# Two-layer transformer kernel: sixteen weighting steps of a batch joined into four, and a new order of all steps

## Chip, cores and metric

The kernel runs on one core of a Trainium2 chip. The metric is device time in microseconds. The engines are TensorE (PE), VectorE (DVE), ScalarE (ACT), GpSimd (POOL) and SyncE (SP), which issues most DMA copies.

## The reference

Sixteen batches of 512 tokens, 128 features, go through four layers: RWKV time and channel mixing; a soft decision tree of depth 8; causal attention with 16 heads of 8 dimensions and rotary positions; a mixture of 16 experts, of which two are picked per token. Each layer's output is added to its input and normalized. What the change touches is the attention's last part:

```python
scores = jnp.einsum('bthd,bshd->bhts', q, k) / jnp.sqrt(jnp.float32(dh))
scores = scores + causal[None, None, :, :]
weights = jax.nn.softmax(scores, axis=-1)
out = jnp.einsum('bhts,bshd->bthd', weights, v).reshape(b, seq, d)
```

## The kernel before

Each engine has a list of named steps in `ORDER`, such as `3:weigh0`. The number ahead of the name is a lag: in turn t of the loop the step works on batch t minus the lag. `run` goes through the list once per turn, so four or five batches are under way at once and an engine does its steps exactly in the written order. Semaphores join the engines: `until(engine, b, name, n)` makes an engine wait until n steps of that name of batch b are done. A step that waits holds up all that stands behind it on its engine.

The steps that matter here:

- `row0` to `row39` (TensorE): scores of queries against keys, in 40 units of up to 512 columns, each a `kh,qh` product and a `maskb,identb` product per piece, into two PSUM banks `S[0]`, `S[1]` in turn. `rowmax` (VectorE) takes the maxima and frees the bank; unit n waits for `rowmax` of unit n - 2. A unit of one piece is followed by the next step 0.28 us after its start, one of two pieces after 0.34 us.
- `score0` to `score39` (TensorE): the same products turned, keys by queries, with the maxima taken off, again into the two banks. `exp0` to `exp39` (ScalarE, line 525) writes the exponentials to one of ten slots of `prob` and frees the bank; unit n waits for `exp` n - 2. `exp` n with n of 10 or more waits for the `weigh` steps that read its slot ten units before.
- `weigh0` to `weigh15` (TensorE, tiles `prob,vaug`): exponentials times values. Step 4g + s handles group g of four heads, for one of the four blocks of keys. Its four matmuls use 32 columns of the array each (`tile_position`). A group needs ten `prob` slots.
- `pvT_out0` and `pvT_out1` (ScalarE) move the weighted sums out after 12 and 16 weighting steps; `back0`, `back1` (TensorE, tiles `ident,pvT`, line 958) turn them; `attend0`, `attend1` (VectorE) divide; then `attT`, `attn_out`.
- Time mixing of a batch two ahead: `k`, `v`, `r`, then `inverse0` to `inverse3` (VectorE reciprocals, line 732), `rwkv0` to `rwkv3` (GpSimd, line 409), `read_out0` to `read_out3` (TensorE, tiles `wo,inner`), `x2` (VectorE, line 742), `moments2`. `read_out0` needs all four `rwkv`.
- Channel mixing: `xn2T`, `cmk0` to `cmk3` (TensorE), each waiting for a `silu` (VectorE) of two before, `cmr`, `cmv0` to `cmv3`.
- Experts of the batch before: `gb0` to `gb15` and `expert0` to `expert15` (TensorE), `u` (VectorE for even numbers, GpSimd for odd ones behind `spread` on ScalarE).
- Rotary heads of the next batch: `xcT`, `rope0` to `rope3` (TensorE), `part_hi`, `part_mid` (ScalarE), `part_lo` (GpSimd), and `heads0`, `heads1` (SyncE): 18 copies each into `qh` and `kh`. `row0` needs all of `heads0`.

Besides these, `xbT`, `gates`, `leafT`, `leaf_sum` belong to the tree of the next batch, whose levels `tree0` to `tree7` are VectorE's; `moments`, `root` and `norm` to the normalizations; `maxT0`, `maxT1` put the maxima into the queries' rows.

Of the kernel before, what the change touches and what calls it, by code (L numbers as in the profile page):

```python
# [28 lines left out]
UNITS = 40  # L29
# [1247 lines left out]
```

How the kernel before makes its waits and increments, by code:

```python
        def until(eng, b, name, n=None):  # L112
            per = PER_BATCH[name]
            if b >= 0:
                eng.wait_ge(sems[name], b * per + (per if n is None else n))
# [1 line left out]
        def reached(eng, name, total):  # L118
            if total > 0:
                eng.wait_ge(sems[name], total)
# [181 lines left out]
        @block.sync  # L303
# [24 lines left out]
            def shared_bias(b):  # L328
                if b == 0:
                    sp.wait_ge(setup["bias_parts"], 7)
                    for i in range(PARTS):
                        sp.dma_start(bias_rows[i:i + 1, :], bias_part[i]).then_inc(setup["bias_in"], 16)
            load(0)
            for dst, src in GAINS:
                sp.dma_start(dst, src, allow_slow_non_contiguous=True).then_inc(setup["gains_in"], 16)
            for dst, src in FIRST[0::2]:
                sp.dma_start(dst, src, allow_slow_non_contiguous=True).then_inc(setup["first_loaded"], 16)
            for dst, src in TIME_LOADS[0:2]:
                sp.dma_start(dst, src, allow_slow_non_contiguous=True).then_inc(setup["time_loaded"], 16)
            for dst, src in LOADS:
                sp.dma_start(dst, src, allow_slow_non_contiguous=True).then_inc(setup["loaded"], 16)
            sp.wait_ge(setup["kh_ones"], 4)
            run("sp", {"load": lambda b: load(b + 1) if b + 1 < B else None, **each("heads", 2, spread_heads), **each("max_rows", 2, spread_maxima), "store": store, "shared_bias": shared_bias})
            until(sp, B - 1, "stored")
```

## Time and profile before

| | |
|---|---|
| median of 3 runs | 1709.79 us (1707.97 to 1712.36) |
| profiled execution | 1714.23 us, its span 1711.8 us |
| busy in the span | PE 1570.9 us, DVE 1418.7, ACT 1025.3, POOL 913.5 |
| mean granted TensorE clock | 0.959 |

The span is the time from the first to the last instruction of the profiled execution. Busy time on one engine can overlap with that on the others; for TensorE, matmuls are pipelined and a matmul's recorded end lies after the start of the next one. Where prices of TensorE's work are needed, differences of starts tell more than durations. A few matmul records are missing from the trace.

### The profile page before, as it was taken

The page shows a single profiled execution, that of the slowest core. Times are in us where ns is not written, and L with a number is a line of the kernel's source. Part 1 is how long each engine was busy: PE and PEld are TensorE (multiplying, and loading weights), DVE is VectorE, ACT ScalarE, POOL GpSimd, SP SyncE. Part 2 cuts the span into 40 slices and gives each one's busy share as a digit, 9 for nine tenths or more (in the row PEclk, how much of TensorE's full clock was granted, in tenths as well). Part 3 has the DMA queues.
Part 4 walks back from the last instruction along what each step waited for, and adds up shares of the span by engine and source line. Part 5 has one row for each costly group of instructions (what it writes and reads, how often), then busy time and mean ns, then how long its engine had stood idle before and what let it go on. Part 6 is the DMA issues. An engine that isn't in the chain of part 4 may idle for free.

```text
span 1711.8 us, 33755 instructions
## 1 busy us (share of the span) xinstructions
PE 1570.9 (92%) x12127; PEld 1094.8 (64%) x12205; DVE 1418.7 (83%) x3018; ACT 1025.3 (60%) x2110; POOL 913.5 (53%) x1233
## 2 busy tenths in 40 slices
PE   3566899999999999999999999999999999999976
PEld 1334558576766758676767768586767767584735
DVE  5776989899898989899998989898998989782612
ACT  3333475766666574857666575757666675746252
POOL 6445264746546574746556564746566474632303
PEclk9687899999999999999999999999999999999897
DMA  4002020110102020100102020201102020201000
GB/s 112 1 6 56 7 57 8 34 31 18 53 8 58 14 56 8 47 24 26 46 8 63 9 57 8 55 17 34 37 13 58 9 57 2 63 2 52 13 14 7
DMA packets 66969, 53.35 MB, mean 31 GB/s; under 512 B 8370, under 2 KB 65522, under 8 KB 66802
## 3 DMA queue, kind: packets, MB, share of 16 engines
q1 hardware_dynamic: 65650, 50.41, 10.7%
q8 instruction: 96, 1.57, 0.4%
q10 hardware_dynamic: 1152, 0.79, 0.2%
q14 instruction: 71, 0.58, 0.1%
HBM read 8.44 MB, written 4.19 MB: 7 GB/s over the span
## 4 chain that ended last, share of the span: by engine, by line
PE 77%; DVE 11%; ACT 3%; issue 3%; SPq 2%; POOL 2%; DMA 1%; another core or an unknown queue 0%; DVEq 0%; ACTq 0%; POOLq 0%
PE bank L962 73%; PE bank L958 4%; SPq L318 2%; DVE rall L788 2%; DVE rall L786 1%; DVE mixed L693 1%; DVE stats L684 1%; DVE rall L784 1%; ACT prob L525 1%; DVE inner L693 1%; DVE wkb L732 1%; DMA kh<-part 1%; DVE xc L814 1%; DVE mv L689 1%; ACT gT L525 0%
## 5 line engine op out<-in xcount | busy, mean ns | idle before, releaser
L525 ACT ACTIVATE prob<-bank 128x512 f32<-128x512 f32 x640 | 355.7, 597 | 131.7 <-PE bank L962 130.0
L962 PEld LDWEIGHTS bank<-wexpT,prob 128*128 128x128 f32 x2048 | 264.7, 193 | 29.2 <-issue 24.9
L962 PE MATMUL bank<-kh,qh 72*128 72x512 bf16 (+3 forms) x1024 | 250.6, 306 | 23.2 <-DVE rall L786 11.2
L962 PE MATMUL bank<-wexpT,prob 128*128 128x128 f32 x2048 | 265.6, 276 | 2.8 <-DVE prob L863 0.3
L461 POOL TENSOR_TENSOR prob<-xdT,spread 128x512 f32<-128x512 f32 x128 | 162.7, 1271 | 192.6 <-ACT spread L525 163.8
L962 PE MATMUL bank<-qh,kh 75*128 75x512 bf16 (+3 forms) x1024 | 242.7, 303 | 6.1 <-ACT prob L525 5.7
L732 DVE RECIPROCAL wkb<-wkb 128x512 f32<-128x512 f32 x64 | 214.0, 3344 | 0.0
L962 PE MATMUL bank<-maskb,identb 128*128 128x128 bf16 x1024 | 192.9, 223 | 0.0
L962 PE MATMUL bank<-maskTb,identb 128*128 128x128 bf16 x1024 | 190.3, 220 | 0.0
L786 DVE TENSOR_REDUCE rall<-bank 128x4 f32<-128x512 f32 x256 | 175.1, 684 | 16.4 <-PE bank L962 15.4
L788 DVE TENSOR_REDUCE rall<-bank 128x1 f32<-128x512 f32 x256 | 174.7, 682 | 16.3 <-PE bank L962 16.1
L395 POOL TENSOR_TENSOR wkb<-wkb,ksum 128x512 f32<-128x512 f32 x64 | 85.5, 1336 | 180.1 <-ACT wkb L525 142.5
L962 PEld LDWEIGHTS bank<-qh,kh 75*128 75x128 bf16 x1024 | 100.2, 98 | 115.1 <-ACT prob L525 70.5
L962 PE MATMUL bank<-prob,vaug 128*32 128x512 f32 (+3 forms) x2048 | 164.4, 445 | 0.0
L525 ACT ACTIVATE spread<-bank 128x512 f32<-128x512 f32 x128 | 76.0, 594 | 143.1 <-PE bank L962 136.4
L962 PEld LDWEIGHTS bank<-kh,qh 72*128 72x128 bf16 x1024 | 102.0, 100 | 92.9 <-DVE rall L786 37.2
L962 PEld LDWEIGHTS bank<-maskTb,identb 128*128 128x128 bf16 x1024 | 101.0, 99 | 34.3 <-issue 33.2
L361 POOL TENSOR_TENSOR var<-mv,eps_ln 128x4 f32<-128x4 f32 x112 | 22.5, 201 | 179.2 <-DVE mv L689 179.2
L365 POOL TENSOR_TENSOR rstd<-var,exponent 128x4 f32<-128x4 f32 x112 | 113.6, 1014 | 1.3
L962 PEld LDWEIGHTS bank<-maskb,identb 128*128 128x128 bf16 x1024 | 102.2, 100 | 14.6 <-issue 9.7
L962 PEld LDWEIGHTS bank<-prob,vaug 128*32 128x32 f32 x2048 | 54.9, 110 | 81.5 <-issue 56.4
L863 DVE TENSOR_TENSOR prob<-xdT,bank 128x512 f32<-128x512 f32 x128 | 86.9, 679 | 19.4 <-PE bank L962 17.2
(213 smaller groups left out, 3477.0 us busy)
## 6 DMA issues: line engine op xcount, KB each, us to landing
qh<-part SPq DMA_DIRECT2D x288, 64.0 KB
kh<-part SPq DMA_DIRECT2D x288, 64.0 KB
x<-in_L_attn_x_dram SPq DMA_DIRECT2D x16, 256.0 KB, 2.8
out_dram<-yo SPq DMA_DIRECT2D x16, 256.0 KB, 2.4
qh<-maxT SPq DMA_DIRECT2D x32, 24.0 KB
wk<-in_L_attn_tm_Wk_dram ACTq DMA_DIRECT2D x1, 256.0 KB, 5.7
wv<-in_L_attn_tm_Wv_dram ACTq DMA_DIRECT2D x1, 256.0 KB, 6.2
wr<-in_L_attn_tm_Wr_dram ACTq DMA_DIRECT2D x1, 256.0 KB, 6.6
```

The source lines that it names most:

```text
L318: sp.dma_start(dst[r:KROWS:PARTS * PARTS, z * NH // 2:(z + 1) * NH // 2, :], part[t][m][half, :]).then_inc(sems[("heads_low", "heads_high" ...
L365: raised(pool.tensor_tensor(rstd[:, n, :], var[:, n, :], exponent[:, :], ALU.pow), f"root{n}")
L395: raised(pool.tensor_tensor(wkb[:, c % 2, :], wkb[:, c % 2, :], ksum[:, c % 2, 0:T], ALU.add), "wk")
L461: raised(pool.tensor_tensor(ug[:, e % 4, :], xdT[:, :], spread[e // 2 % 2][:, :], ALU.mult), "ug_side")
L525: raised(act.activation(dst, src, func, **kw), signal)
L693: return dve.scalar_tensor_tensor(out=out_, in0=in0, scalar=scalar, in1=in1, op0=op0, op1=op1)
L732: raised(dve.reciprocal(wkb[:, c % 2, :], wkb[:, c % 2, :]), "wk_inv")
L786: last = dve.tensor_reduce(rall[:, 0:PARTS + 1, h], S[n % 2].rearrange("p (z s) -> p z s", z=J), AX_X, ALU.max)
L788: last = dve.tensor_reduce(rmax[:, PLACE[3], h:h + 1], S[n % 2], AX_X, ALU.max)
L863: raised(dve.tensor_tensor(ug[:, e % 4, :], xdT[:, :], G, ALU.mult), "ug")
L958: last = pe.transpose(bk[:, j * P:(j + 1) * P], t[:, j, :], ident[:, :])
L962: return pe.matmul(out_, w, x, start=start, stop=stop, **kw)
```

## The change

The four weighting steps of a group of four heads become one step, `weighs0` to `weighs3`, with the same matmuls in the same order and the same waits between them:

```diff
@@ -1141,6 +1141,10 @@
+            def weigh_group(b, g):
+                for k in range(4 * g, 4 * g + 4):
+                    weigh(b, k)
+
@@ -1216,7 +1220,7 @@
-                **each("row", UNITS, row_scores), **each("maxT", 2, turn_maxima), **each("score", UNITS, scores), **each("weigh", 16, weigh),
+                **each("row", UNITS, row_scores), **each("maxT", 2, turn_maxima), **each("score", UNITS, scores), **each("weighs", NQ, weigh_group),
```

and the lists of TensorE, ScalarE, VectorE and GpSimd are written anew (SyncE's stays). They begin at another point of the loop, so that lags of most steps are one less, while each step works on the same batch as before relative to its neighbours. Of TensorE's list:

```diff
-        2:leafT1 3:score4 3:score5 1:r2 3:maxT1 3:score6 3:score7 2:leaf_sum 3:score8 3:score9 3:weigh0 3:weigh1 3:weigh2 3:score10 3:score11
+        2:score4 0:k2 1:leafT1 2:score5 2:score6 0:r2 2:score7 2:score8 1:leaf_sum 2:score9 2:score10 2:weighs0 2:score11 2:score12 0:k3 2:score13
+        2:score14 2:maxT1 2:score15 0:v3 2:score16 2:score17 0:r3 2:score18 2:score19 2:weighs1 2:score20 1:xcT 2:score21 2:score22 1:rope0 1:rope1
```

Of ScalarE's list, around `pvT_out0`, and of VectorE's, around `x2`:

```diff
-        3:pvT_out0 3:exp32 2:part_hi1 3:exp33 3:exp34 2:part_mid1 3:exp35 3:exp36 3:exp37 3:exp38 3:exp39 0:norm0 3:pvT_out1 1:norm2 3:attT_out
+        0:r_tanh3 2:exp21 2:exp22 2:exp23 2:exp24 2:exp25 2:exp26 1:part_hi0 2:exp27 2:exp28 2:exp29 0:weights 1:part_mid0 2:exp30 2:pvT_out0 2:exp31
+        2:exp32 2:exp33 1:part_hi1 2:exp34
-        4:moments7 1:x2 1:moments2 3:attend0 2:rowmax0 1:weights 2:rowmax1 3:attend1 2:rowmax2 2:rowmax3 2:rowmax4 2:rowmax5 1:mix3 3:yc 1:mix4
+        1:inverse2 2:rope_mul2 2:rope_mul3 1:inverse3 1:weights 4:moments7 0:moments0 3:attend0 1:x2 1:moments2 2:rowmax0 3:attend1 2:rowmax1
```

Places in TensorE's program, for one batch in the middle. First, the scores ahead of the third group of heads. A `qh,kh` row with its mask row is a piece; banks 4 and 5 are `S[0]` and `S[1]`; `xbT,w_rope` is `rope3`. Before, from `rope3` on:

```order
L962 MATMUL bank3<-xbT,w_rope 128x512
L962 MATMUL bank4<-qh,kh 128x384
L962 MATMUL bank4<-maskTb,identb 128x128
L962 MATMUL bank4<-qh,kh 128x128
L962 MATMUL bank4<-maskTb,identb 128x128
L962 MATMUL bank5<-qh,kh 128x256
L962 MATMUL bank5<-maskTb,identb 128x128
L962 MATMUL bank5<-qh,kh 128x256
L962 MATMUL bank5<-maskTb,identb 128x128
L962 MATMUL bank6<-prob,vaug 32x512 x4
L962 MATMUL bank6<-prob,vaug 32x384 x4
L962 MATMUL bank6<-prob,vaug 32x128 x4
```

After, from `score27` on, which now stands behind `rope3`:

```order
L962 MATMUL bank5<-qh,kh 128x512
L962 MATMUL bank5<-maskTb,identb 128x128
L962 MATMUL bank4<-qh,kh 128x384
L962 MATMUL bank4<-maskTb,identb 128x128
L962 MATMUL bank4<-qh,kh 128x128
L962 MATMUL bank4<-maskTb,identb 128x128
L962 MATMUL bank5<-qh,kh 128x256
L962 MATMUL bank5<-maskTb,identb 128x128
L962 MATMUL bank5<-qh,kh 128x256
L962 MATMUL bank5<-maskTb,identb 128x128
L962 MATMUL bank4<-qh,kh 128x512
L962 MATMUL bank4<-maskTb,identb 128x128
```

Two units, `score28` and `score29`, stood between `rope3` and the weighting steps; now four, `score27` to `score30`, stand between them.

Second, the steps from `back0` (`ident,pvT`) to the read-outs (`wo,inner`). Before:

```order
L958 MATMUL bank7<-ident,pvT 128x128 x4
L962 MATMUL bank4<-qh,kh 128x256
L962 MATMUL bank4<-maskTb,identb 128x128
L962 MATMUL bank4<-qh,kh 128x256
L962 MATMUL bank4<-maskTb,identb 128x128
L962 MATMUL bank1<-wo,inner 128x128 x4
L962 MATMUL bank5<-qh,kh 128x512
L962 MATMUL bank5<-maskTb,identb 128x128
L962 MATMUL bank1<-wo,inner 128x128 x8
```

After:

```order
L958 MATMUL bank7<-ident,pvT 128x128 x4
L962 MATMUL bank5<-qh,kh 128x384
L962 MATMUL bank5<-maskTb,identb 128x128
L962 MATMUL bank5<-qh,kh 128x128
L962 MATMUL bank5<-maskTb,identb 128x128
L962 MATMUL bank4<-qh,kh 128x256
L962 MATMUL bank4<-maskTb,identb 128x128
L962 MATMUL bank4<-qh,kh 128x256
L962 MATMUL bank4<-maskTb,identb 128x128
L962 MATMUL bank5<-qh,kh 128x512
L962 MATMUL bank5<-maskTb,identb 128x128
L962 MATMUL bank1<-wo,inner 128x128 x12
```

`score33` has moved behind `back0`, and `score35` ahead of the first read-out, so that three units adjoin.

Third, the last weighting step of a batch and the first rows (`kh,qh` with `maskb`) of the next. Before:

```order
L962 MATMUL bank6<-prob,vaug 32x256 x4
L962 MATMUL bank4<-kh,qh 128x512
L962 MATMUL bank4<-maskb,identb 128x128
L962 MATMUL bank5<-kh,qh 128x384
L962 MATMUL bank5<-maskb,identb 128x128
L962 MATMUL bank5<-kh,qh 128x128
L962 MATMUL bank5<-maskb,identb 128x128
L958 MATMUL bank7<-ident,pvT 128x128 x4
L962 MATMUL bank4<-kh,qh 128x512
L962 MATMUL bank4<-maskb,identb 128x128
```

After:

```order
L962 MATMUL bank6<-prob,vaug 32x256 x4
L962 MATMUL bank4<-kh,qh 128x512
L962 MATMUL bank4<-maskb,identb 128x128
L958 MATMUL bank7<-ident,pvT 128x128 x4
L962 MATMUL bank5<-kh,qh 128x384
L962 MATMUL bank5<-maskb,identb 128x128
L962 MATMUL bank5<-kh,qh 128x128
L962 MATMUL bank5<-maskb,identb 128x128
L962 MATMUL bank4<-kh,qh 128x512
L962 MATMUL bank4<-maskb,identb 128x128
L958 MATMUL bank7<-ident,att 128x128 x4
```

`back1` now stands behind the first unit of rows, where it stood behind the second; one unit fewer stands ahead of `attT` (`ident,att`).

## Rows read from the trace of the kernel before

**Rows 1.** The page: busy us of each engine (share of the span), instructions.
```profile
PE 1570.9 (92%) x12127; PEld 1094.8 (64%) x12205; DVE 1418.7 (83%) x3018; ACT 1025.3 (60%) x2110; POOL 913.5 (53%) x1233
```

**Rows 2.** TensorE's timeline, 719.9 to 726 us: start, duration, operation, count.
```profile
720.09 0.22 PE L962 MATMUL bank<-maskTb,identb 128*128 128x128 bf16 x1
720.24 2.36 PE L962 MATMUL bank<-prob,vaug 128*32 128x512 f32 x32
722.53 0.39 PE L962 MATMUL bank<-kh,qh 72*128 72x512 bf16 x1
...
722.82 0.33 PE L962 MATMUL bank<-kh,qh 72*128 72x384 bf16 x1
...
723.41 0.63 PE L958 MATMUL bank<-ident,pvT 128*128 128x128 f32 x4
```

**Rows 3.** TensorE's timeline at the start of the next batch's rows.
```profile
817.84 0.39 PE L962 MATMUL bank<-kh,qh 72*128 72x512 bf16 x1
```

**Rows 4.** One batch: window, length, busy of PE, PEld, DVE, ACT, POOL, clock.
```profile
722.53:817.84 95.31, 93.81 (x760) 66.69 (x761) 87.47 (x188) 63.27 (x131) 56.02 (x76) 1.00 0.12 32
```

**Rows 5.** TensorE's waits from 722 to 818 us: total, times, longest.
```profile
PE bank L962 <- DVE rall L786: 0.6, 1, 0.6
```

**Rows 6.** TensorE's timeline, 728.5 to 733 us.
```profile
731.35 0.34 PE L962 MATMUL bank<-kh,qh 72*128 72x384 bf16 x1 [0.56 <-DVE rall L786]
...
731.94 0.28 PE L962 MATMUL bank<-kh,qh 72*128 72x256 bf16 x1
...
732.53 0.70 PE L962 MATMUL bank<-mixed,cwk 128*128 128x512 f32 x1
```

**Rows 7.** VectorE's timeline, 719.9 to 726 us.
```profile
719.67 0.69 DVE L742 TENSOR_TENSOR x<-x,bank 128x512 f32<-128x512 f32 x1 [3.98 <-PE bank L962]
...
723.02 0.69 DVE L788 TENSOR_REDUCE rall<-bank 128x1 f32<-128x512 f32 x1 [0.25 <-PE bank L962]
723.62 0.68 DVE L786 TENSOR_REDUCE rall<-bank 128x4 f32<-128x512 f32 x1
```

**Rows 8.** TensorE's timeline, 709.1 to 715 us.
```profile
712.10 0.33 PE L962 MATMUL bank<-qh,kh 75*128 75x384 bf16 x1
...
713.44 0.34 PE L962 MATMUL bank<-qh,kh 75*128 75x384 bf16 x1
...
713.93 0.66 PE L958 MATMUL bank<-ident,pvT 128*128 128x128 f32 x4
...
714.79 0.38 PE L962 MATMUL bank<-wo,inner 128*128 128x128 f32 x1
```

**Rows 9.** GpSimd's timeline, 704 to 719.5 us.
```profile
713.46 1.28 POOL L409 TENSOR_TENSOR inner<-rth,wkb 128x512 f32<-128x512 f32 x1 [0.16 <-DVE wkb L732]
...
716.85 1.16 POOL L437 TENSOR_TENSOR part<-tree,part 128x512 bf16<-128x512 f32 x1 [0.74 <-ACT part L525]
```

**Rows 10.** VectorE's timeline, 704 to 719.5 us.
```profile
710.04 3.35 DVE L732 RECIPROCAL wkb<-wkb 128x512 f32<-128x512 f32 x1
```

**Rows 11.** TensorE's timeline, 688 to 694.2 us.
```profile
690.39 0.22 PE L962 MATMUL bank<-maskTb,identb 128*128 128x128 bf16 x1
690.54 1.93 PE L962 MATMUL bank<-prob,vaug 128*32 128x512 f32 x24
692.41 0.39 PE L962 MATMUL bank<-qh,kh 75*128 75x512 bf16 x1
...
692.97 0.22 PE L962 MATMUL bank<-maskTb,identb 128*128 128x128 bf16 x1
...
693.69 0.39 PE L962 MATMUL bank<-qh,kh 75*128 75x512 bf16 x1
```

**Rows 12.** ScalarE's timeline, 712 to 716 us.
```profile
712.30 1.08 ACT L525 ACTIVATE prob<-bank 128x512 f32<-128x512 f32 x2 [0.97 <-PE bank L962]
713.27 0.60 ACT L525 ACTIVATE pvT<-bank 128x512 f32<-128x512 f32 x1
```

**Rows 13.** The copies that SyncE issues, 705 to 725 us.
```profile
714.90 5.86 SPq L318 DMA_DIRECT2D kh<-part  x9
```

More of the change, by code:

```diff
@@ L69 @@
-        1:weights 1:mix_before3 1:mix_before4 4:norm7 1:cmk_tanh0 1:cmk_tanh1 3:norm6 1:cmk_tanh2 3:xdT_out 1:cmk_tanh3 2:norm4 3:route_exp 2:values
-        1:cmr_tanh 3:gate_hi 3:gate_mid 3:gT_out 0:norm1 3:spread1 0:mix_before0 3:spread3 0:mix_before1 0:mix_before2 2:max_hi0 3:spread5 1:norm3
-        2:max_mid0 2:max_lo0 2:maxT_out0 3:spread7
+        2:part_mid1 3:exp35 3:exp36 3:exp37 3:exp38 3:exp39 3:pvT_out1 1:norm2 3:attT_out 1:mix_before3 1:mix_before4 0:norm0 4:norm7 1:cmk_tanh0
+        1:cmk_tanh1 3:norm6 1:cmk_tanh2 3:xdT_out 1:cmk_tanh3 3:route_exp 2:norm4 1:cmr_tanh 3:gate_hi 2:values 3:gate_mid 3:gT_out 3:spread1 0:norm1
@@ new lines @@
+        3:spread3 3:spread5 0:mix_before0 0:mix_before1 2:max_hi0 0:mix_before2 2:max_mid0 2:vaug 2:max_lo0 3:spread7 2:maxT_out0 3:spread9 1:norm3
+        0:k_exp0 1:xbT_out 3:spread11 0:k_first0 1:gate0 0:r_tanh0 1:gate1 3:spread13 0:k_exp1 3:spread15 0:r_tanh1 0:k_first1 2:exp0 2:exp1 2:exp2
+        2:exp3 1:leafT_out0 2:exp4 2:exp5 2:exp6 1:leafT_out1 2:exp7 2:max_hi1 0:k_exp2 2:exp8 2:max_mid1 2:exp9 0:k_first2 2:exp10 0:r_tanh2 2:exp11
+        2:exp12 2:max_lo1 2:exp13 2:exp14 2:maxT_out1 2:exp15 0:k_exp3 2:exp16 2:exp17 0:k_first3 2:exp18 2:exp19 1:norm_rms 2:exp20 1:xcT_out
@@ new lines @@
+        2:rowmax2 2:rowmax3 2:rowmax4 1:mix3 3:yc 1:mix4 3:moments6 2:rowmax5 2:rowmax6 1:silu0 2:rowmax7 2:rowmax8 1:silu1 2:rowmax9 1:silu2
+        2:rowmax10 1:silu3 3:route_logits 3:largest0 3:route_probs 3:others 3:largest1 2:rowmax11 2:rowmax12 2:rowmax13 0:moments1 2:rowmax14
+        2:rowmax15 3:u0 2:rowmax16 2:rowmax17 3:u2 2:rowmax18 2:rowmax19 1:y0 2:rowmax20 2:max_join0 3:u4 2:rowmax21 2:rowmax22 1:moments3 3:u6
+        2:rowmax23 2:rowmax24 0:mix0 2:rowmax25 3:u8 0:mix1 0:mix2 2:rowmax26 2:rowmax27 0:clamp0 2:rowmax28 2:rowmax29 3:u10 0:kv0 2:rowmax30
@@ L90 @@
-        3:weigh8 3:weigh9 3:weigh10 3:score30 3:score31 3:weigh11 3:score32 3:score33 3:back0 3:score34 1:read_out0 3:score35 1:read_out1 1:read_out2
-        3:score36 3:score37 1:read_out3 3:score38 3:score39 3:weigh12 3:weigh13 3:weigh14 3:weigh15 2:row0 2:row1 1:weights 3:back1 2:row2 2:row3
-        3:attT 1:xn2T 2:row4 2:row5 3:attn_out 2:attn_v 2:row6 2:row7 1:cmk0 1:cmk1 2:row8 2:row9 1:cmk2 2:row10 2:row11 3:xdT 1:cmk3 3:centroids
-        1:cmr 2:row12 3:shared 1:cmv0 1:cmv1 2:row13 1:cmv2 2:row14 2:row15 1:cmv3 3:gT 2:row16 2:row17 3:gb0 3:biases 2:row18 3:gb1 3:expert0 3:gb2
@@ L94 @@
-        0:xnT 2:row19 2:row20 3:gb3 3:expert1 3:gb4 3:expert2 2:row21 2:row22 3:gb5 3:expert3 2:row23 2:row24 3:gb6
+        3:back1 2:row1 2:row2 3:attT 1:xn2T 2:row3 2:row4 3:attn_out 2:attn_v 2:row5 2:row6 1:cmk0 1:cmk1 2:row7 2:row8 1:cmk2 2:row9 2:row10 3:xdT
+        1:cmk3 2:row11 3:centroids 1:cmr 2:row12 3:shared 1:cmv0 1:cmv1 2:row13 1:cmv2 2:row14 2:row15 3:gT 1:cmv3 2:row16 3:gb0 2:row17 3:biases
+        3:gb1 3:expert0 3:gb2 2:row18 2:row19 3:gb3 3:expert1 2:row20 2:row21 3:gb4 3:expert2 2:row22 3:gb5 0:xnT 3:expert3 3:gb6 3:expert4 2:row23
@@ new lines @@
+        2:row24 3:gb7 3:expert5 2:row25 2:maxT0 3:gb8 3:expert6 2:row26 2:row27 3:gb9 3:expert7 0:k0 2:row28 2:row29 3:gb10 3:expert8 0:v0 1:xbT
+        2:row30 2:row31 3:gb11 0:r0 3:expert9 2:row32 2:row33 3:gb12 1:gates0 1:gates1 3:expert10 2:row34 0:k1 2:row35 3:gb13 3:expert11 2:row36
+        3:gb14 3:expert12 0:v1 2:row37 2:row38 3:gb15 3:expert13 2:row39 0:r1 3:expert14 3:expert15 2:score0 2:score1 0:v2 2:score2 2:score3 1:leafT0
+        2:score4 0:k2 1:leafT1 2:score5 2:score6 0:r2 2:score7 2:score8 1:leaf_sum 2:score9 2:score10 2:weighs0 2:score11 2:score12 0:k3 2:score13
@@ L95 @@
+        2:score14 2:maxT1 2:score15 0:v3 2:score16 2:score17 0:r3 2:score18 2:score19 2:weighs1 2:score20 1:xcT 2:score21 2:score22 1:rope0 1:rope1
+        2:score23 2:score24 1:rope2 2:score25 2:score26 1:rope3 2:score27 2:score28 2:score29 2:score30 2:weighs2 2:score31 2:score32 0:weights
+        2:back0 2:score33 2:score34 2:score35 0:read_out0 0:read_out1 0:read_out2 2:score36 2:score37 0:read_out3 2:score38 2:score39 2:weighs3
+        1:row0
     """,
```

27 lines of the change are left out of this document (7 added, 20 removed).

## The prediction

> **What bounds the kernel now.** I read the page's busy shares first, then one batch in the middle. TensorE is busy 92% of the span and VectorE 83%, ScalarE 60% [rows 1]. The loop is steady: the first `row` unit of a batch starts at 722.53 us and that of the next at 817.84 us, 95.3 us later [rows 2, 3]. In that batch TensorE is busy 93.8 of 95.3 us at a granted clock of 1.00, which is the 2.4 GHz level, VectorE 87.5, ScalarE 63.3 [rows 4]. The view of waits names only 0.6 us of TensorE's time for the longest wait in that batch [rows 5]. So TensorE's own queue sets the period, and VectorE comes close behind it. What each engine has left is spent in small waits that this view doesn't count (it leaves out gaps that end before an earlier matmul's recorded end): they are read from the starts of TensorE's rows. I find some 3 us of them in a batch, of which about 1.2 us stand at `row8` (731.35, where 730.62 was due), `row9` (731.94, due 731.69) and `cmk2` (732.53, due 732.28) [rows 6], where VectorE is late. VectorE has one large hole, 4.0 us ahead of `x2` [rows 7], where it waits for `read_out3`. `read_out0` in turn starts at 714.79 [rows 8], just after GpSimd's last `rwkv`, from 713.46 for 1.28 us [rows 9], which needed VectorE's last reciprocal, from 710.04 for 3.35 us [rows 10]. So a second chain (VectorE's packed row from the maxima to `inverse3`, then GpSimd, then the read-outs) has only 0.05 us of room beside TensorE's queue. A change must help both to shorten the period; it lengthens the period as soon as either gets longer.
>
> **1. Fewer changes between the two kinds of matmul.** The 32-column matmuls of `weigh` now stand in seven blocks per batch (0-2, 3, 4-6, 7, 8-10, 11, 12-15), afterwards in four. The prices are differences of starts [rows 11]. A mask matmul of 128 columns is followed by the next one 0.06 us later in plain order. Ahead of `weigh0` the last starts at 690.39, so the block of three costs 692.41 - 690.45 = 1.96 us. Likewise the lone `weigh3` costs 693.69 - 693.03 = 0.66 us. Together that is 2.62 us. The four in one block, as `weigh12` to `weigh15` already run, cost 722.53 - 720.15 = 2.38 us [rows 2]. So each joining saves 0.24 us, three of them 0.7 us a batch, and nothing hides it, since TensorE's queue is packed. The Trainium skill, "TensorEngine Tiling (Array Packing)", Key Properties, says that changing the tiling mode drains TensorE, which by itself speaks for this change. What it makes of the time is the first rival.
>
> **2. The scores in the new order.** A score unit may start when the `exp` two units before it has emptied its bank. The loop is read from [rows 8, 12]: `score31` starts at 712.10 and its masks end 0.50 us later (0.44 for a unit of one piece); `exp31` is the second of the two that begin at 712.30 and end at 713.38; `score33` starts at 713.44. One `exp` lasts 0.60 us, the next starts 0.48 after it, and each handover takes about 0.05. So the third of three adjoining units can start no earlier than 0.44 to 0.50 + 0.05 + 0.60 + 0.05 = about 1.16 us after the first, while two units take TensorE only 0.28 to 0.34 us each, 0.62 together. Now every pair is followed by other work of at least 0.5 us; the new order breaks this:
> - `score27` to `score30` adjoin. `score29` waits 1.16 - 0.62 = 0.54 us, `score30` 0.48 - 0.34 = 0.14: 0.7 us. `weighs2` can't fill them, it stands behind `score30`.
> - After `weighs2` come `score31`, `score32`, `back0`, then `score33` to `score35`. `pvT_out0` now stands ahead of `exp31` on ScalarE. From the start of `score31` its end is 0.07 + 0.06 + 0.60 = 0.73 us, so `back0` (due at 0.62) waits 0.16; `exp32` ends at 1.69 and `score34` (due at 1.61) waits 0.13; `score35` needs `exp33`, which begins after `score33` ends, and waits 0.39. That is 0.7 us; it delays `read_out0`, now behind `score35`.
> - `score15` has only `maxT1` (0.22 us) between it and the pair before: 0.3 us. `score4` has only `leafT0` (0.44): 0.1 us. `rope0` waits about 0.2 for `xcT_out`, which stands behind `exp20`.
> - Gone are today's waits of `score13` (0.07), `score33` (0.06: 713.44, due 713.38), `back0` (0.15: 713.93, due 713.78) and `read_out0` (0.03): 0.3 us.
>
> Together 0.7 + 0.7 + 0.3 + 0.1 + 0.2 - 0.3 = 1.7 us a batch. I take it whole. Its lower bound is 0.7, with the four adjoining scores and nothing else; its upper bound is 2.0, with nothing gone.
>
> **3. The first rows of the next batch.** Now `row0` and `row1` stand ahead of `back1`. `row1` begins at 722.82 and takes 0.34 us, so `back1` is due at 723.16; it starts at 723.41 [rows 2] and has waited 0.25 for `pvT_out1`. Afterwards only `row0` (0.28 us) stands there; `pvT_out1` comes no sooner after the block, so `back1` still starts 0.88 us after `row0` and the wait is 0.6. `row1`, behind it, gives VectorE its unit later: `rowmax1` followed `rowmax0` 0.60 us on [rows 7], and now VectorE has nothing to do until `attend1`. `attT` then waits for `attend1` as today. What is queued behind: `xn2T`, all rows of the batch, `cmk0`. Followed down both queues with today's durations, TensorE is 0.3 us later at `row12`, gets 0.1 back where `gT_out` no longer makes it wait, and reaches `score0` 0.2 us later than today; VectorE is 1.3 us later at its last tree level, because it waits for `gb0`, `gb2` and `row23` too. I take +0.2 us for TensorE, between -1.2 (all of today's waits at `row8`, `row9`, `cmk2` vanish) and +0.6 (VectorE's lost unit counts whole). VectorE's delay is no second price: with `rope0` at its new place, `inverse3` ends about 1.1 us later than today and `rwkv3` with it, just ahead of the `read_out0` that part 2 has delayed. It means that part 2 has no slack to vanish in.
>
> **4. Moved at no price.** `attend0` goes ahead of `x2`, into the 4.0 us hole [rows 7], and had room behind it before too. `moments1`, `norm1`, `xnT`, `norm3`, `xbT` move later by 1 to 8 us; what needs them (`mix0`, `gates0`) moves with them, and were the cover gone `xbT` would cost its 0.44. The expert steps come 1.5 to 2 us earlier against `k0`. SyncE's list is the same: its 18 copies of the heads leave 0.65 us apart (nine in 5.86 us [rows 13]), after `part_mid0`, and the last part is ready at 718.01 (716.85 + 1.16 [rows 9]), 4.5 us ahead of `row0`. With `part_hi1` behind `exp33` this chain slips by about 1.3 us against 1.1 for `row0`; `back1`'s wait covers the difference. The weights' preparation of batch 0 goes ahead of its read-outs; I count 0 for it, plus or minus 2 us in all.
>
> **Sum.** -0.7 + 1.7 + 0.2 = +1.2 us a batch. Some 14 of 16 batches run fully overlapped: +17 us, 1.0%. On the profiled execution, 1714.2 us (its span 1711.8 and 2.4 around it), that gives 1731; that execution lies 4.4 us over the median of the three runs, 1709.8, so I predict 1727.
>
> **The rivals.**
> - *Only the changes of mode count.* If the new waits of part 2 fall into time that TensorE loses anyway, three switches less in 16 batches give 16 x 0.7 = 11 us: 1699, faster. That is the rule of the Trainium skill's "TensorEngine Tiling (Array Packing)" taken alone. For it: TensorE is the bound [rows 4] and the saving can't hide. Against it: the loop of 1.16 us in [rows 8, 12]. It decides if the waits of parts 2 and 3 together are under 0.5 us. Chance 0.17.
> - *The waits in the row stage go.* `moments1`, 1.2 us of VectorE, no longer stands between `silu1` and `silu2`, and a row fewer is asked for early. If the 1.2 us at `row8`, `row9` and `cmk2` vanish, the sum is about 0.0 a batch: 1708 to 1712, no change. Against it: `moments6` and both `mix` steps stand ahead of `silu0` as before. Chance 0.18.
> - *The heads come late.* If the copies, not `pvT_out1`, set `row0`, another 0.5 us is lost a batch: 1734. Against it: today's 4.5 us from the last part to `row0` are also the least that TensorE's queue allows, so the copies may need less. Chance 0.1.
> - My forecast, 1715 to 1733: 0.55.
>
> **How the numbers follow.** A difference of 0.3%, 5 us, is what can be told from none. Faster is the first rival and little else, 0.17; same is the second, 0.18; slower is the forecast and the third, 0.65. The range leaves out the fast half of the first rival and what is beyond the third: 1702 to 1736. The forecast's own range is 1715 to 1733, from part 2's lower bound (with part 3 at 0.4 us) to its upper.
>
> **What would show it.** Right: a period near 96.5 us; four blocks of 32-column matmuls of about 2.4 us each; a start of `score29` over 1.1 us after `score27`; `score35` at least 0.6 us after `score34`; `back1` 0.9 us after `row0`. Wrong: a period under 95 us, with those units 0.3 us apart because `exp` was quicker or the work ahead later than I set it, or `silu0` and `row8` without a wait.

## The result, and the profile after

| | before | after |
|---|---|---|
| median of 3 runs | 1709.79 us (1707.97 to 1712.36) | 1736.11 us (1731.96 to 1736.34) |
| profiled execution | 1714.23 us, span 1711.8 | 1736.11 us, span 1733.2 |
| mean granted TensorE clock | 0.959 | 0.962 |

The changed kernel is slower: ratio 1.014, interval 1.012 to 1.017. The medians differ by 26.3 us, the two profiled executions by 21.9.

The page after the change, busy us of each engine; it answers to [rows 1].

```profile
PE 1581.5 (91%) x12205; PEld 1093.7 (63%) x12205; DVE 1432.7 (83%) x3018; ACT 1025.7 (59%) x2110; POOL 929.3 (54%) x1233
```

VectorE is busy 14 us longer and GpSimd 16, with the same instructions. (TensorE's 10.6 us more come with 78 more matmul records, which the trace before lacks.) That is the first hint: operations there became longer.

Batches no longer all take the same time. Two in a row by the view of windows, from one first `row0` to the next (length, then busy time and count of PE, PEld, DVE, ACT and POOL, then clock); they answer to [rows 4]:

```profile
727.24:825.05 97.81, 95.02 (x762) 66.79 (x762) 89.14 (x186) 63.58 (x131) 57.37 (x77) 1.00 0.11 31
825.05:921.56 96.51, 94.59 (x761) 66.66 (x762) 88.06 (x186) 62.91 (x131) 57.20 (x75) 1.00 0.11 32
```

Of the thirteen batches from the second `row0` to the fifteenth, five take 96.5 to 96.6 us and eight take 97.5 to 98.0. Before, twelve of them took 95.3 to 95.8 and the last 97.1. The two kinds have two causes, read one after the other.

**The short batches** are the ones that the prediction worked out. TensorE's timeline of the batch from 825.05 us (start, duration, operation, count, and in brackets an idle time with what ended it):

```profile
825.05 0.39 PE L962 MATMUL bank<-kh,qh 72*128 72x512 bf16 x1 [0.56 <-DMA kh<-part]
...
825.33 0.60 PE L958 MATMUL bank<-ident,pvT 128*128 128x128 f32 x4
...
889.29 2.36 PE L962 MATMUL bank<-prob,vaug 128*32 128x512 f32 x32
891.58 0.34 PE L962 MATMUL bank<-qh,kh 75*128 75x384 bf16 x1
...
906.75 0.38 PE L962 MATMUL bank<-qh,kh 75*128 75x512 bf16 x1
...
907.88 0.28 PE L962 MATMUL bank<-qh,kh 75*128 75x256 bf16 x1 [0.35 <-ACT prob L525]
...
912.80 0.28 PE L962 MATMUL bank<-qh,kh 75*128 75x256 bf16 x1
...
913.51 0.39 PE L962 MATMUL bank<-qh,kh 75*128 75x512 bf16 x1 [0.20 <-ACT prob L525]
```

A block of four weighting steps holds the queue 2.29 us from start to start. `score27` starts at 906.75 and `score29` 1.13 us later. `score34` starts at 912.80 and `score35` 0.71 later. So the loop of the exponentials is as the prediction reads it in [rows 8, 12].

**The long batches** have a cost that the prediction has not. VectorE's timeline around `tree4` (two instructions of 64 columns), first in a long batch, then in a short one:

```profile
778.57 0.68 DVE L788 TENSOR_REDUCE rall<-bank 128x1 f32<-128x512 f32 x1
779.17 1.59 DVE L693 SCALAR_TENSOR_TENSOR tree<-tree 128x64 f32<-128x64 f32 x2
780.69 0.68 DVE L786 TENSOR_REDUCE rall<-bank 128x4 f32<-128x512 f32 x1
...
876.33 0.68 DVE L788 TENSOR_REDUCE rall<-bank 128x1 f32<-128x512 f32 x1
876.93 0.48 DVE L693 SCALAR_TENSOR_TENSOR tree<-tree 128x64 f32<-128x64 f32 x2
877.32 0.69 DVE L786 TENSOR_REDUCE rall<-bank 128x4 f32<-128x512 f32 x1
```

GpSimd's timeline at the same two places, where it runs `u15`:

```profile
779.42 1.27 POOL L461 TENSOR_TENSOR prob<-xdT,spread 128x512 f32<-128x512 f32 x1 [2.42 <-ACT spread L525]
...
877.18 1.36 POOL L461 TENSOR_TENSOR prob<-xdT,spread 128x512 f32<-128x512 f32 x1 [2.41 <-ACT spread L525]
```

In the long batch `u15` starts 0.25 us after `tree4`, as the second of its two instructions begins, and that one ends at 780.76, 0.07 us after `u15`: `tree4` takes 1.59 us, not 0.48. In the short batch `u15` starts 0.25 us after `tree4` too; `tree4` keeps its 0.48 us, and `u15` is the one that is 0.09 us longer. So one of the two holds the other up, and it is VectorE's that pays heavily: it waits until GpSimd's is over. The Trainium skill, "SBUF — State Buffer", section "SBUF: two separate sides", states a rule for it: an operation of VectorE with two inputs in SBUF and one of GpSimd that reads SBUF take turns at a pair of ports that they share, and whichever starts first holds it for the whole instruction. The rows agree: the tree operation reads two SBUF tensors and waits, and the row maximum that runs beside `u15` in the short batch (877.32) reads PSUM and keeps its 0.69 us.

`tree4` has 1.59 us in eight of the thirteen batches, the eight long ones. What decides is below a hundredth of a microsecond. In all thirteen `u15` is recorded 0.244 to 0.246 us after the start of `tree4`, and the second tree instruction 0.249 to 0.251: in the short batches `u15` stands 0.004 us ahead of it, in the long ones 0.006 to 0.007. The recorded order is thus the same in both kinds; which of the two took hold first, the records don't show. Where `tree4` stands in its batch doesn't tell the two kinds apart: 51.89 to 51.97 us after `row0` in the short ones, 51.89 to 51.96 in the long.

VectorE's 1.1 us reach TensorE at two steps: in the long batches `leafT0` makes it 0.30 us late, and `r2` brings that to 0.92 (medians of starts after `row0`). From the last block on it is 1.03. TensorE's timeline at `r2`, which waits for `clamp2` of VectorE:

```profile
788.35 1.13 PE L962 MATMUL bank<-mixed,wr 128*128 128x512 f32 x2 [0.47 <-DVE kk L706]
```

**The sum of both.** From the second to the fifteenth `row0`, thirteen batches, there are 1241.9 us before and 1264.2 after: 22.3 us of difference, against 21.4 in the span. Thirteen times 96.55 - 95.32 = 1.23 is 16.0 us. Eight times 1.05 is 8.4. The odd single batches (2.7 us over the regular period before, 0.6 after) take 2.1 back. In these `row0` waits longer for the copies of the heads: 1.75 us in the last of the thirteen before, where the regular ones have no such wait. Such batches occur in most of the runs below, and the periods given there leave them out.

### The profile page after: what moved, and what is told of

It is laid out like the page before. It is cut to its first block, busy times and chain, and to the rows that moved or that the text cites. A ratio compares the mean times of both kernels' runs of the same rounds, so it can differ in the third digit from the quotient of the medians.

```text
span 1733.2 us, 33833 instructions
## 1 busy us (share of the span) xinstructions
PE 1581.5 (91%) x12205; PEld 1093.7 (63%) x12205; DVE 1432.7 (83%) x3018; ACT 1025.7 (59%) x2110; POOL 929.3 (54%) x1233
## 4 chain that ended last, share of the span: by engine, by line
PE 65%; DVE 17%; SPq 5%; ACT 5%; issue 4%; DMA 2%; POOL 1%; DVEq 0%; ACTq 0%; POOLq 0%
PE bank L962 61%; SPq L318 5%; PE bank L958 4%; ACT prob L525 2%; DVE tree L693 2%; DVE rall L786 2%; DMA kh<-part 2%; DVE rall L788 1%; DVE mixed L693 1%; ACT part L525 1%; DVE stats L684 1%; DVE prob L863 1%; DVE rall L784 1%; DVE ksum L719 1%; DVE kvsum L724 1%
## 5 line engine op out<-in xcount | busy, mean ns | idle before, releaser
L962 PE MATMUL bank<-wexpT,prob 128*128 128x128 f32 x2048 | 270.2, 276 | 0.2 <-POOL prob L461 0.2
L962 PE MATMUL bank<-qh,kh 75*128 75x512 bf16 (+3 forms) x1024 | 247.6, 304 | 17.8 <-ACT prob L525 14.5
L461 POOL TENSOR_TENSOR prob<-xdT,spread 128x512 f32<-128x512 f32 x128 | 167.4, 1308 | 168.3 <-ACT spread L525 168.1
L395 POOL TENSOR_TENSOR wkb<-wkb,ksum 128x512 f32<-128x512 f32 x64 | 115.7, 1807 | 255.3 <-DVE ksum L719 255.3
L962 PE MATMUL bank<-prob,vaug 128*32 128x512 f32 (+3 forms) x2048 | 155.6, 445 | 0.0
```

Of the source, the lines that this page charges most:

```text
L395: raised(pool.tensor_tensor(wkb[:, c % 2, :], wkb[:, c % 2, :], ksum[:, c % 2, 0:T], ALU.add), "wk")
L461: raised(pool.tensor_tensor(ug[:, e % 4, :], xdT[:, :], spread[e // 2 % 2][:, :], ALU.mult), "ug_side")
L962: return pe.matmul(out_, w, x, start=start, stop=stop, **kw)
```

## Experiments

Diffs show the lists of one engine, cut to the place; a batch number ahead of a step is left as in the list.

### The joining alone, in the old order

```diff
 pe
-3:weigh2 3:score10 3:score11 3:weigh3 3:score12
+3:weigh2 3:weigh3 3:score10 3:score11 3:score12
-3:weigh6 2:xcT 1:r3 ... 3:score23 3:weigh7 3:score24
+3:weigh6 3:weigh7 2:xcT 1:r3 ... 3:score23 3:score24
-3:weigh10 3:score30 3:score31 3:weigh11 3:score32
+3:weigh10 3:weigh11 3:score30 3:score31 3:score32
 act
-3:exp18 2:norm_rms 3:exp19
+3:exp18 3:exp19 2:norm_rms
```

> The old order with the weighting steps joined in place: weigh3, weigh7 and weigh11 move up behind weigh2, weigh6 and weigh10, and exp19 goes ahead of norm_rms so that weigh7 finds it done; nothing else. My theory: each joining saves the 0.24 us that two blocks cost more than one, up to 0.7 us a batch, less where read_out0 then waits for rwkv3; 6 to 11 us faster than before, 1699 to 1704. Rival: it is the joined step itself that costs time, since slots of prob come free later: slower than before, with waits of score12 and score22.

Measured: 1732.03 us (1730.62 to 1737.01), ratio 1.013, interval 1.011 to 1.016. My theory fell: three blocks less a batch cost 1.27 us instead of saving 0.7. All batches but three odd ones take 96.6 us, and none has the long `tree4`. TensorE's timeline at the second place where a step went, around `score22` to `score25`:

```profile
903.64 0.38 PE L962 MATMUL bank<-qh,kh 75*128 75x512 bf16 x1
...
903.92 0.33 PE L962 MATMUL bank<-qh,kh 75*128 75x384 bf16 x1
...
904.77 0.28 PE L962 MATMUL bank<-qh,kh 75*128 75x256 bf16 x1 [0.35 <-ACT prob L525]
...
905.26 0.39 PE L962 MATMUL bank<-qh,kh 75*128 75x512 bf16 x1
```

`weigh7` was what filled the time between two pairs of scores. Without it `score24` starts 1.13 us after `score22`, where 0.62 was due, and `score25` 0.49 after that, where 0.34 was due. That happens at each of the three places. Followed by starts, TensorE is 0.42 us later than before at `score14`, 0.91 at `score26`, 1.33 at `back0`, and gets 0.07 back behind `read_out0`. Each place loses about 0.67 us of waits and gains 0.24.

### One place alone

```diff
 pe
-3:weigh2 3:score10 3:score11 3:weigh3 3:score12
+3:weigh2 3:weigh3 3:score10 3:score11 3:score12
```

> The kernel before with one step moved: weigh3 directly behind weigh2, so that only the first group is in one piece. Theory of the lost filler: the block takes 0.24 us less, but score10 to score13 now stand side by side and score12 waits about 0.6 us for the exponentials, in all 0.4 us a batch more: 1714 to 1718 us. Rival, only the change of kind counts: 0.24 us a batch less, 1706 to 1708 us. A third outcome: the 0.4 us are taken up before read_out0, where the RWKV chain does not depend on it, and the time stays within 2 us of before.

Measured: 1719.03 us, ratio 1.0046, interval 1.0033 to 1.0058. The period is 95.73 us, 0.42 more than before, as the theory of the lost filler says; 14 batches make 6 us, inside the interval (5.6 to 9.9 us). The place in TensorE's timeline:

```profile
882.34 2.36 PE L962 MATMUL bank<-prob,vaug 128*32 128x512 f32 x32
884.64 0.39 PE L962 MATMUL bank<-qh,kh 75*128 75x512 bf16 x1
...
884.92 0.33 PE L962 MATMUL bank<-qh,kh 75*128 75x384 bf16 x1
...
885.77 0.39 PE L962 MATMUL bank<-qh,kh 75*128 75x512 bf16 x1 [0.35 <-ACT prob L525]
...
886.26 0.34 PE L962 MATMUL bank<-qh,kh 75*128 75x384 bf16 x1
```

`score12` starts 1.13 us after `score10`, `score13` 0.49 later, and from there to `row0` everything is late by the same 0.43 us: TensorE's queue has no slack that takes it up.

### The lost filler put back

```diff
 pe
-3:weigh2 3:score10 3:score11 3:weigh3 3:score12 3:score13 1:v2 3:score14 3:score15 1:k3
-3:score16 3:score17 1:v3 3:score18 3:score19 3:weigh4 3:weigh5 3:weigh6 2:xcT 1:r3
+3:weigh2 3:weigh3 3:score10 3:score11 1:v2 3:score12 3:score13 1:k3 3:score14 3:score15 1:v3
+3:score16 3:score17 1:r3 3:score18 3:score19 3:weigh4 3:weigh5 3:weigh6 2:xcT
```

> The kernel before with weigh3 directly behind weigh2, as in the kernel that took 1719 us, and in addition v2, k3, v3 and r3 each moved up by one pair of scores, so that other matmuls stand behind every pair again. Theory, joining as such saves 0.24 us a block and it was only the lost filler that cost 0.67: the period falls to 95.1 us or just stays at 95.3 where the second chain holds it, 1706 to 1711 us, at least 8 us under the kernel that only joined. Rival, the filler is no explanation (the block itself or its length of 2.3 us without a score costs): 1715 us or more.

Measured: 1720.64 us, ratio 1.0065, interval 1.0044 to 1.0086, 95.9 us a batch. By its time my theory lost. The trace shows why it isn't refuted: the new order brought two waits of its own. TensorE's timeline:

```profile
889.13 1.12 PE L962 MATMUL bank<-mixed,wv 128*128 128x512 f32 x2
...
894.35 0.66 PE L958 MATMUL bank<-ident,xch 128*128 128x128 f32 x4
894.84 0.38 PE L962 MATMUL bank<-qh,kh 75*128 75x512 bf16 x1
...
895.12 0.33 PE L962 MATMUL bank<-qh,kh 75*128 75x384 bf16 x1
...
896.01 0.70 PE L962 MATMUL bank<-xbT,w_rope 128*128 128x512 f32 x1 [0.39 <-ACT xbT L525]
```

`score12` to `score19` no longer wait. At `score20`, with the same work done on both sides, TensorE stands where it stood before (75.22 us after `row0`, 75.23 before), 0.43 us ahead of a mere joining and 0.24 short of the gain, of which `v3` lost 0.20 (it waited for `kv2`). But `r3` no longer stands behind `xcT`, which starts 0.86 us later than before, and `rope0` (896.01) now waits 0.55 us for `xcT_out`. That the waits of the scores go when their cover returns is shown. That a joined block then makes a faster kernel is not; a version without the two new waits was not run.

### Is it TensorE's queue or the second chain?

A much shorter operation in place of `inverse3`, in the kernel before, in the one with all three joined, and in the changed one.

```diff
-raised(dve.reciprocal(wkb[:, c % 2, :], wkb[:, c % 2, :]), "wk_inv")
+if c == 3:
+    last = dve.tensor_scalar(wkb[:, c % 2, :], wkb[:, c % 2, :], 0.0, 0.0, ALU.mult, ALU.add)
+else:
+    last = dve.reciprocal(wkb[:, c % 2, :], wkb[:, c % 2, :])
+raised(last, "wk_inv")
```

> The kernel before, with the last of the four reciprocals of a batch (inverse3, 3.35 us on VectorE) replaced by a much shorter operation that writes zeros, so that the last quarter of the RWKV part is not computed rightly. The baseline of this call. Before, read_out0 starts as rwkv3 ends, and the matmul queue reaches it at almost the same time (0.05 us of room). Theory, the queue of TensorE sets the period: 95.3 us a batch, 1709 to 1712 us. Rival, the chain of VectorE and GpSimd sets it and TensorE only follows: more than 0.3 us a batch shorter, under 1705 us.

> The order of before with the three weighting steps moved up to their groups (the kernel that took 1732 us), and the same short operation in place of inverse3. Theory, the steps that stood between two pairs of scores covered the loop of the exponentials, and without them scores wait on TensorE: the period stays within 0.2 us of 96.59, 1729 to 1733 us. Rival, joining costs because the block of four stands ahead of xcT and makes the rope products, inverse2, inverse3 and rwkv3 0.92 us late: then read_out0 comes early now, the period falls to 95.2 to 95.7, 1709 to 1717 us.

> The changed kernel with the same short operation in place of inverse3. In its batches of 96.6 us read_out0 starts at 88.75 us, right behind score35, and rwkv3 ends at 88.57. Theory, scores that wait in the new order hold TensorE: the short batches stay at 96.4 to 96.6, the long ones (tree4 waits for GpSimd) at 97.4 to 97.6, in all 1731 to 1736 us. Rival, the late chain of VectorE and GpSimd holds it: 95.6 to 96.1 and 1720 to 1727 us.

Measured: 1708.62 us (ratio 0.999, interval 0.998 to 1.000), 1731.53 (1.0121, 1.0106 to 1.0136) and 1738.99 (1.0166, 1.0152 to 1.0181); periods 95.25, 96.57 and 97.7. In the first two it is TensorE's queue that sets the period. GpSimd's last `rwkv` and TensorE's `read_out0`, in the kernel with all three joined and the short operation:

```profile
910.14 1.26 POOL L409 TENSOR_TENSOR inner<-rth,wkb 128x512 f32<-128x512 f32 x1
```

```profile
912.08 0.77 PE L966 MATMUL bank<-wo,inner 128*128 128x128 f32 x5
```

The last `rwkv` ends at 911.40, and TensorE comes to `read_out0` at 912.08: 0.68 us of room, and the period is the same to 0.02 us. In the kernel before, the room of 0.05 us is about the 0.07 us that its period loses. The third run decides nothing for the changed kernel, and it came out above what either theory said. `tree4` takes 1.59 us in every batch. And `rwkv3` did not come earlier with its input: it stands close behind the rope sum in GpSimd's queue, which is itself a little later. GpSimd's last `rwkv` and TensorE's `read_out0` there:

```profile
916.04 1.27 POOL L409 TENSOR_TENSOR inner<-rth,wkb 128x512 f32<-128x512 f32 x1
```

```profile
917.36 0.82 PE L966 MATMUL bank<-wo,inner 128*128 128x128 f32 x5
```

It ends at 917.31, 0.05 us ahead of `read_out0`, which was due at 917.29 behind `score35` (917.01): here TensorE waits for the second chain. In the changed kernel itself `rwkv3` ends 0.18 us ahead of `read_out0` in short and long batches, so that chain isn't what holds it, but it is close.

### The wait of tree4 for GpSimd

Two ways past it in the changed kernel, `tree4` ahead of `rowmax37`, or `kv1` behind `tree4`:

```diff
 dve (first)
-0:kv1 2:rowmax37 1:tree4 2:rowmax38
+0:kv1 1:tree4 2:rowmax37 2:rowmax38
 dve (second)
-0:kv1 2:rowmax37 1:tree4 2:rowmax38
+2:rowmax37 1:tree4 0:kv1 2:rowmax38
```

> The changed kernel with one step moved: tree4 ahead of rowmax37 on VectorE. In the changed kernel's trace tree4 takes 1.59 us instead of 0.48 in about half of the batches, those in which GpSimd's u15 has begun before it, and those batches last 97.6 us instead of 96.6. If that clash is the cause, all batches last 96.6 us, 7 to 10 us faster than the changed kernel: 1726 to 1729. Rival: tree4 is only late because of something else in those batches; then two kinds of batches stay and the time is the same.

> The changed kernel with one step of VectorE's list moved: kv1 behind rowmax37 and tree4 instead of ahead of them. tree4 then ends about 0.15 us before GpSimd's u15 starts, where it now misses it by 0.04 us in most batches and waits 1.1 us for the end of u15. Theory, this wait is the term that the prediction lacks: all batches take 96.5 to 96.6 us and the time is 1724 to 1729 us, 8 to 11 us under the changed kernel. Rival, the wait goes to kv1 or to another operation beside u15: 97 us or more a batch, 1733 us or more.

Measured: 1733.39 us (ratio 1.013, interval 1.011 to 1.015) and 1727.27 us (1.0109, 1.0087 to 1.0131). Both have `tree4` at 0.48 us in every batch and one period instead of two: 96.88 and 96.7 us, but for single odd batches. The first pays for it, since `rowmax37` ends 0.5 us later and TensorE's `row39` with it (0.33 us later), and it missed the expected 1726 to 1729. The second takes the wait out at 0.15 us a batch. VectorE's and GpSimd's timelines in the second:

```profile
871.33 0.69 DVE L788 TENSOR_REDUCE rall<-bank 128x1 f32<-128x512 f32 x1 [0.20 <-PE bank L962]
871.94 0.48 DVE L693 SCALAR_TENSOR_TENSOR tree<-tree 128x64 f32<-128x64 f32 x2
872.34 0.68 DVE L712 TENSOR_TENSOR kvb<-kk,bank 128x512 f32<-128x512 f32 x1
```

```profile
872.56 1.27 POOL L461 TENSOR_TENSOR prob<-xdT,spread 128x512 f32<-128x512 f32 x1 [2.42 <-ACT spread L525]
```

`tree4` ends 0.14 us before `u15` starts, and what stands beside `u15` (`kv1`, a maximum) has no more than one input in SBUF. That this wait makes the long batches is shown. Its worth in the whole time is less sharp. The median is 8.8 us under that of the changed kernel, measured in another set of runs; against the kernel before in its own set, the change costs 18.3 us where it cost 26.3. In the traces the thirteen batches take 5.2 us less (1259.0 against 1264.2): 8.4 for the wait, less 2.0 for the 0.15 a batch and 1.2 for odd batches.

### Cutting the groups again in the new order

```diff
 pe
-2:weighs0 2:score11 2:score12
+2:weigh0 2:weigh1 2:weigh2 2:score11 2:weigh3 2:score12
-2:weighs1 2:score20 1:xcT 2:score21
+2:weigh4 2:weigh5 2:weigh6 2:score20 2:weigh7 1:xcT 2:score21
-2:weighs2 2:score31 2:score32
+2:weigh8 2:weigh9 2:weigh10 2:score31 2:weigh11 2:score32
```

> The new order with the first three groups cut again: three weighting steps, one score unit, the fourth step. Seven blocks a batch as before the change. My theory: 0.24 us more for each cut where TensorE's queue sets the end, 0.7 us a batch, 5 to 10 us slower than the changed kernel: 1741 to 1746. Less if VectorE's chain to rwkv3 sets the end of the score stage: then as slow as the changed kernel. Rival (the joined step costs the time): 15 us or more faster than the changed kernel.

Measured: 1756.15 us, ratio 1.0267, interval 1.0252 to 1.0283; 98.5 us in every batch. Against the changed kernel's long batches that is 0.95 us. By starts, TensorE is 0.28 us later at `k3`, another 0.24 at `xcT` and another 0.58 at `back0`, of which it gets 0.15 back in between. The third cut costs more than the change of kind. `pvT_out0` needs `weigh11`, so it comes later on ScalarE, and `back0` waits for it in TensorE's timeline:

```profile
920.37 0.64 PE L962 MATMUL bank<-prob,vaug 128*32 128x256 f32 x8
920.94 0.39 PE L962 MATMUL bank<-qh,kh 75*128 75x512 bf16 x1
...
921.73 0.66 PE L958 MATMUL bank<-ident,pvT 128*128 128x128 f32 x4 [0.34 <-ACT pvT L525]
```

Another 5 of the 20 us are `tree4`: here it takes 1.59 us in all thirteen batches, not in eight. So in the new order the joining does help, by about 0.24 us at the first and second group and more at the third. And the waits of the adjoining scores stay when the groups are cut: `score29` again starts 1.13 us after `score27`.

```profile
917.20 0.28 PE L962 MATMUL bank<-qh,kh 75*128 75x256 bf16 x1 [0.35 <-ACT prob L525]
```

### The old end of the scores in the new order

From `score25` on, TensorE's and ScalarE's lists in the order of before, with the third group cut as before (`score25 rope2 score26 score27 rope3 score28 score29`, then `weigh8` to `weigh10`, and so on).

> The new order, but from score25 on TensorE's and ScalarE's lists have the old order up to score39 (pairs of scores between rope2, rope3, weigh8-10, weigh11, back0, read_out0). If TensorE's waits for the banks at score29, score30, score34, score35 set the time, some 1.0 us a batch comes back (1.4 less 0.24 for the cut and the old waits): 14 us faster than the changed kernel, 1722. Rival within my theory: in the changed kernel's trace rwkv3 ends only 0.1 to 0.2 us ahead of read_out0, so VectorE's chain is just as late; then the units come 0.3 us apart, read_out0 waits for rwkv3 instead, and the time falls by 0 to 4 us: 1732 to 1736.

Measured: 1738.11 us, ratio 1.0161, interval 1.0141 to 1.0182; 96.86 us in the short batches and 97.86 in the long ones. The four adjoining scores are gone, and the time isn't. `score25` now stands third in a row and waits; this row of TensorE's timeline is it:

```profile
908.12 0.39 PE L962 MATMUL bank<-qh,kh 75*128 75x512 bf16 x1 [0.35 <-ACT prob L525]
```

`score28` waits another 0.20: `exp26` stands behind `part_hi0` on ScalarE, which here comes late from GpSimd. The cut costs its 0.24. And `read_out0` waits 0.20 us for the second chain; GpSimd's last `rwkv` and TensorE's `read_out0`, due at 916.77:

```profile
915.65 1.27 POOL L409 TENSOR_TENSOR inner<-rth,wkb 128x512 f32<-128x512 f32 x1
```

```profile
916.97 1.16 PE L962 MATMUL bank<-wo,inner 128*128 128x128 f32 x8
```

The waits were moved, in part by one pair and in part to the rival's place, not removed.

### Matmuls of rope between the scores

On top of `kv1` behind `tree4`:

```diff
 pe
-1:rope0 1:rope1 2:score23 2:score24 1:rope2 2:score25 2:score26 1:rope3 2:score27 2:score28 2:score29 2:score30
+1:rope0 2:score23 2:score24 1:rope1 2:score25 2:score26 1:rope2 2:score27 2:score28 1:rope3 2:score29 2:score30
```

> The kernel with kv1 behind tree4, and in addition rope1, rope2 and rope3 moved down by a pair of scores each on TensorE, so that no four scores adjoin between score27 and score30. It tests the largest term of part 2 of the prediction, 0.7 us a batch for these four. Theory, the scores no longer wait there (0.5 and 0.15 us in the trace), but rope_mul1 and with it inverse2, inverse3 and rwkv3 come 0.6 us later, and read_out0 waits for rwkv3 instead: the same time within 3 us. Rival, this chain has room now: 0.6 us a batch less, 8 us. Other rival, the rope parts make the heads late and row0 waits: slower by more than 3 us.

Measured: 1736.65 us, ratio 1.0155, interval 1.0132 to 1.0179, 97.43 us a batch, 9 us more than the kernel it starts from. No rival had the mechanism whole. TensorE's timeline at `score29` and at `read_out0`:

```profile
909.26 0.28 PE L962 MATMUL bank<-qh,kh 75*128 75x256 bf16 x1 [0.30 <-ACT prob L525]
...
915.69 0.49 PE L962 MATMUL bank<-wo,inner 128*128 128x128 f32 x2 [0.35 <-POOL inner L409]
```

TensorE is 0.68 us ahead at `score27`. Then `score29` waits 0.47 us longer than its due start, because `exp27` stands behind `part_hi0` on ScalarE, and that waits for GpSimd, where the rope sums are later. After it, `read_out0` waits for `rwkv3`. The rope steps feed the second chain and so don't serve as cover here.

### The heads, and the order of the first rows

On top of `kv1` behind `tree4`:

```diff
 act
-2:exp33 1:part_hi1 2:exp34
+1:part_hi1 2:exp33 2:exp34
 pe
-3:back1 2:row1 2:row2
+2:row1 3:back1 2:row2
```

> The kernel with kv1 behind tree4, and in addition part_hi1 ahead of exp33 (the heads' last part is ready earlier) and back1 behind row1 instead of ahead of it. row0 now waits 0.35 us for the copies of the heads, then back1 0.2 us for pvT_out1. Theory, both waits end at the same pvT_out1, and with both edits only 0.25 of the 0.55 us are left: 0.3 us a batch less than the kernel it starts from, 4 to 5 us. Rival, the heads are late for another reason (their copies queue behind others), row0 waits as before: within 2 us of it. If exp33 behind part_hi1 makes score35 and read_out0 late, it is slower by up to 5 us.

Measured: 1727.51 us, ratio 1.0108, interval 1.0087 to 1.0130: no change against 1727.27. TensorE's timeline over the last block and the first rows:

```profile
917.83 2.36 PE L962 MATMUL bank<-prob,vaug 128*32 128x512 f32 x32
920.12 0.39 PE L962 MATMUL bank<-kh,qh 72*128 72x512 bf16 x1
...
920.99 0.63 PE L958 MATMUL bank<-ident,pvT 128*128 128x128 f32 x4
...
922.30 0.33 PE L958 MATMUL bank<-ident,att 128*128 128x128 f32 x1 [0.40 <-DVE att L808]
```

The heads are no longer late: `row0` follows its block by 2.29 us, where it took 2.69 in the changed kernel. Yet `back1` starts 3.16 us after the start of that block and `attT` 4.47. In the changed kernel these are 3.17 and 4.47, and in the kernel before 3.17 and 4.61. So the chain `pvT_out1`, `back1`, `attend1`, `attT` fixes this stretch in the new order, and whether `row1` stands ahead of `back1`, or the copies of the heads are 0.4 us late, changes nothing. What `part_hi1` took from `exp33` (`read_out0` 0.3 us later) used up the rest.

## Why the prediction came out as it did

- **Direction and size.** Slower was right. 1736.1 us lie 9 us over the predicted 1727 and at the very edge of the range (1736). The failing step is **the sum**, which has no term for VectorE and GpSimd excluding each other. Part 3 followed VectorE's queue with "today's durations". But `tree4`, 50.3 us after `row0` before and 51.9 now, lands on `u15` (51.8 before, 52.1 to 52.2 now), and its duration is no longer today's: 1.59 us for 0.48 in eight batches, 1.05 us a batch. With this wait out, the kernel took 1727.3 us, 18.3 over the kernel before in the same set of runs, where +17 was said. That 1736.1 still falls on the edge of the range is luck: this end was set for heads that come late (1734), and they cost nothing.
- **Part 1** was right on the price. 0.24 us a join shows in the old order (0.67 us of waits, 0.43 net), and 0.24 to 0.28 at the first two cuts in the new one.
- **Part 2** was right as a sum and in its items. From `score0` to the last block, TensorE takes 38.64 us instead of 37.70: +0.94, where -0.7 and +1.7 give 1.0. `score29` came 1.13 us after `score27` (1.16 was said), `score35` 0.71 after `score34` (0.39 of wait and 0.34), `score4` 0.07 late, `rope0` 0.14. In this order they are the order's waits, as it said: cutting the groups again leaves them in place. What it didn't see is that the saving of part 1 can't be had without some such price. With nothing else changed the joining makes waits of its own, in other places, and costs 1.27 us a batch, by chance about as much as the whole change costs in a short batch. Which order has a joined block and no waits stays open.
- **Part 3.** From the start of the last block to the next `score0`, 57.87 us against 57.61: +0.26, +0.2 was said. `back1` was to wait from 0.88 us after `row0`; it starts 0.48 after it in most batches and 0.28 in the one shown, since `row0` itself is late, by 0.4 us in most batches, for the copies of the heads. The rival "The heads come late" thus had its cause right and its 0.5 us wrong: the wait lies under that of `pvT_out1`.
- **Part 2's remark on slack.** `rwkv3` ended just ahead of `read_out0` (88.57 and 88.75 us after `row0`), as said: 0.18 us of room, and the run without the four adjoining scores then waited for it.
- **"Only the changes of mode count"** failed on its own condition. It needed the costs of parts 2 and 3 under 0.5 us together; they come to 1.9 (the 1.20 above and the 0.7 of part 1). In the old order, with parts 2 and 3 away, it failed too: 0.67 us of waits a join.
- **"The waits in the row stage go"** didn't happen. By starts against what was due, `row7` waits 0.66 us now, `row8` 0.32 and `cmk2` 0.25, together 1.2, as `row8`, `row9` and `cmk2` did before [rows 6].

## What to carry to other kernels

Before work of one kind is gathered into one block, ask what the pieces did where they stood: in the old order each lone weighting step covered about 0.66 us of a loop between TensorE and ScalarE, and its 0.24 us of switching was the cheap part. When a step moves on VectorE or GpSimd, its duration can change too: list which of its operations read two SBUF tensors and what the other engine runs at the new time. And where a period comes in two sizes, look for an operation with two durations: here it was a race between two engines.

## What the runs showed of the hardware that I had not expected

An operation of VectorE with two SBUF inputs waited for a running GpSimd operation to its end (1.59 us instead of 0.48). In a fixed program the batches split on it: with `u15` recorded 0.004 us ahead of the second tree instruction a batch took 96.5 to 96.6 us, with 0.006 to 0.007 it took 97.5 or more. Such waits were there before the change too, at other operations: a product of VectorE's (`kvb,first,kvsum`) that starts 0.28 us after one of GpSimd's takes 1.39 us in sixteen places, and 0.7 elsewhere. The busy time that VectorE and GpSimd gained is not `tree4` alone: a scan of VectorE's (`kvsum`) went from 1.21 to 1.40 us on average and an operation of GpSimd's (`wkb,ksum`) from 1.34 to 1.81, while that product fell from 0.90 to 0.71. The period of the short batches is accounted for without any of this.
